# Moving four token normalisations from VectorE to ScalarE in a two-layer transformer kernel

## What is computed

```
def _layernorm(x, axis=-1, eps=1e-05):
    m = jnp.mean(x, axis=axis, keepdims=True)
    v = jnp.var(x, axis=axis, keepdims=True)
    return (x - m) / jnp.sqrt(v + eps)

x = x + _L0_attn_ref(_layernorm(x), ...)   # 16 heads of 8, gated relative position bias
x = x + _L0_ffn_ref(_layernorm(x), ...)    # router, 4 of 16 experts, and a shared expert
x = x + _L1_attn_ref(_layernorm(x), ...)   # 8 heads of rank 64
x = x + _L1_ffn_ref(_layernorm(x), ...)    # feed-forward with FP4-rounded x and weights
```

## Time and profile before

| what | value |
|---|---|
| runs | 2324.96, 2321.24, 2319.95 us |
| median | 2321.24 us |
| profiled execution: its time | 2319.1 us |
| profiled execution: its span | 2317.3 us |
| granted TensorE clock, mean | 0.947 of full speed |
| busy, share of the span | PE 88%, DVE 70%, ACT 56%, POOL 43% |

### The profile page before, as it was taken

The page is one execution under the profiler, slowest core; times in us unless marked ns, Lnnn a source line. Parts: engine busy times, 40 slices in busy tenths (PEclk is TensorE's granted clock), DMA queues, the critical chain, the costliest instruction groups (busy, mean ns, idle before and its releaser), DMA issues. The chain is left out here.

```text
span 2317.3 us, 56731 instructions
## 1 busy us (share of the span) xinstructions
PE 2037.8 (88%) x18115; PEld 1061.5 (46%) x18115; DVE 1625.4 (70%) x3414; ACT 1308.5 (56%) x2072; POOL 1000.9 (43%) x867
## 2 busy tenths in 40 slices
PE   5569999999999999983999759999999999998566
PEld 3434444444444444453555323444444444443345
DVE  4778888888888888866544676666666666664696
ACT  2236666666666666642222346777778787877121
POOL 1133222322322332421000226787878787877454
PEclk9779999999999999976999988999999999999787
DMA  5522212221222221100000271111111111100000
GB/s 134 149 62 56 53 48 53 54 50 50 55 52 48 54 54 49 37 11 1 1 0 0 92 232 36 42 31 38 34 34 37 31 38 31 41 14 1 1 14 23
DMA packets 126924, 106.60 MB, mean 46 GB/s; under 512 B 39636, under 2 KB 102724, under 8 KB 126860
## 3 DMA queue, kind: packets, MB, share of 16 engines
q1 hardware_dynamic: 124640, 103.37, 16.8%
q10 hardware_dynamic: 2220, 2.45, 0.4%
HBM read 75.81 MB, written 29.53 MB: 45 GB/s over the span
## 5 line engine op out<-in xcount | busy, mean ns | idle before, releaser
L1049 DVE TENSOR_REDUCE b_mx<-psum 128x1 f32<-128x512 f32 x1024 | 663.9, 686 | 143.3 <-PE psum L868 81.0
L1033 ACT ACTIVATE b_prob<-psum 128x1024 f32<-128x1024 f32 x512 | 523.9, 1023 | 317.9 <-PE psum L900 317.8
L1736 POOL TENSOR_TENSOR f_plo<-f_prob,f_phi 128x512 f16<-128x512 f32 x512 | 586.5, 1156 | 164.4 <-ACT f_phi L1861 140.1
L1879 DVE TENSOR_REDUCE f_mx<-psum 128x1 f32<-128x512 f32 x512 | 328.7, 683 | 169.1 <-PE psum L1756 168.1
L1860 ACT ACTIVATE f_prob<-psum 128x512 f32<-128x512 f32 x512 | 307.3, 600 | 150.8 <-PE psum L1767 149.7
L948 PE MATMUL psum<-b_prob,b_v 128*32 128x256 f32 x4096 | 327.4, 391 | 1.6 <-ACT b_prob L1033 0.5
L1861 ACT ACTIVATE f_phi<-psum 128x512 f16<-128x512 f32 x512 | 306.0, 598 | 0.0
L804 POOL COPY b_v<-v 128x64 f32 x64 | 15.1, 236 | 596.1 <-PE psum L948 595.7
L900 PE MATMUL psum<-b_diag,b_toep 128*128 128x79 f16 (+1 forms) x4224 | 266.6, 208 | 0.0
L807 POOL TENSOR_TENSOR b_diag<-flip,grev 128x1024 f16<-128x1024 f16 x128 | 239.6, 1892 | 0.0
L900 PEld LDWEIGHTS psum<-b_diag,b_toep 128*128 128x128 f16 x4224 | 235.2, 99 | 9.0 <-issue 2.6
(11 more groups left out here) (301 smaller groups left out, 3432.4 us busy)
## 6 DMA issues: line engine op xcount, KB each, us to landing
d_qk<-e_qk SPq DMA_DIRECT2D x64, 256.0 KB, 2.6
b_toep<-d_line SPq DMA_DIRECT2D x128, 64.0 KB
f_qa<-d_qk SPq DMA_DIRECT2D x64, 128.0 KB, 2.9
f_ka<-d_qk SPq DMA_DIRECT2D x64, 128.0 KB, 2.9
b_q<-d_q SPq DMA_DIRECT2D x128, 54.0 KB
d_k<-a_qk SPq DMA_DIRECT2D x48, 128.0 KB, 2.3
b_toep<-d_line SPq DMA_DIRECT2D x128, 32.0 KB
b_q<-b_m SPq DMA_DIRECT2D x256, 1.0 KB
```

The source lines that it names most:

```text
L1033: nc.scalar.activation(prob[:, t % 4, :].rearrange("p (a n) -> p a n", a=2), ps[:, EXP + 2 * (t % 2):EXP + 2 * (t % 2) + 2, :], ACT.Exp).t ...
L1049: nc.vector.tensor_reduce(mx[:, b, t, half:half + 1], ps[:, bank, :], AX.X, ALU.max).then_inc(s.max_read, 1)
L1736: nc.gpsimd.tensor_tensor(plo[:, t % 4, at], prob[:, t % 4, at], phi[:, t % 4, at], ALU.subtract).then_inc(s.plo_ready, 1)
L1879: nc.vector.tensor_reduce(mx[:, b, t, half:half + 1], ps[:, MAX + half, :], AX.X, ALU.max).then_inc(s.max_read, 1)
```

## The change

The statistics stay on DVE. POOL forms, beside rstd, a shift of -mean * rstd (two more products of 128 x 4). ACT applies the normalisation as one ACTIVATE with the function Identity per tile, with rstd as scale and shift as bias, both per partition: rstd * x + shift. DVE's four TENSOR_SCALARs per chunk go. `norm_stats` gets a wait before it overwrites `mv`, `norm_rstd` one before it overwrites rstd and shift. A third constant row (-1.0) is set once.

```
 def norm_stats(nc, ln, x, n, u, link, dve, rstd_ready, var_ready):
     for k in reversed(range(CT)):
         last = nc.vector.bn_stats(...)
     link(last)
+    dve.wait_ge(rstd_ready, done(n - 2))
     nc.vector.memset(ln.gap[:, :], 0.0)

 def norm_rstd(nc, g, ln, pool, n, u, s):
     pool.wait_ge(s.var_ready, done(n))
+    pool.wait_ge(s.xn_ready, done(n - 2))
     nc.gpsimd.tensor_tensor(ln.rstd[:, u, :], ln.mv[:, u, :, 1], g.lnc[:, 0, :], ALU.add).then_inc(s.eps_added, 1)
+    nc.gpsimd.tensor_tensor(ln.shift[:, u, :], ln.mv[:, u, :, 0], g.lnc[:, 2, :], ALU.mult)
     pool.wait_ge(s.eps_added, done(2 * n))
     nc.gpsimd.tensor_tensor(ln.rstd[:, u, :], ln.rstd[:, u, :], g.lnc[:, 1, :], ALU.pow).then_inc(s.eps_added, 1)
+    pool.wait_ge(s.eps_added, done(2 * n + 1))
+    nc.gpsimd.tensor_tensor(ln.shift[:, u, :], ln.shift[:, u, :], ln.rstd[:, u, :], ALU.mult).then_inc(s.rstd_ready, 1)

-def norm_apply(nc, ln, x, n, u, xn_ready):
+def norm_apply(nc, ln, x, n, u, act, rstd_ready, xn_ready):
+    act.wait_ge(rstd_ready, done(n))
     for k in range(CT):
-        last = nc.vector.tensor_scalar(ln.xn[:, u, k, :], x[...], ln.mv[:, u, k, 0:1], ln.rstd[:, u, k:k + 1], ALU.subtract, ALU.mult)
+        last = nc.scalar.activation(ln.xn[:, u, k, :], x[...], ACT.Identity,
+                                    bias=ln.shift[:, u, k:k + 1], scale=ln.rstd[:, u, k:k + 1])
     last.then_inc(xn_ready, 1)

 # phase_project0, ACT (and apply(n + 1, 1 - u) gone from DVE's step)
+                act.wait_ge(g.x_loaded, 16)
+                apply(0, 0)
                 move_xT(0, 0)
                 def step(n, u, last):
+                    if not last:
+                        apply(n + 1, 1 - u)
                     act.wait_ge(s.gates_psum, done(n))

 # phase_output0
-                pipeline(act, [(4, move_xT), (1, move_aT), (5, score)])
+                pipeline(act, [(4, move_xT), (1, move_aT), (3, normalise), (5, score)])
-                pipeline(dve, [(2, add_stats), (3, normalise)])
+                pipeline(dve, [(2, add_stats)])

 # phase_project1
-                pipeline(act, [(2, lambda n, u: high(n, u, FIRST)), (1, move_xT), (2, lambda n, u: high(n, u, REST))])
+                pipeline(act, [(1, normalise), (2, lambda n, u: high(n, u, FIRST)), (1, move_xT), (2, lambda n, u: high(n, u, REST))])
-                pipeline(dve, [(1, normalise), (2, lambda n, u: low(n, u, FIRST)), (1, low_xT), (0, stats),
+                pipeline(dve, [(2, lambda n, u: low(n, u, FIRST)), (1, low_xT), (0, stats),

 # phase_quant_ffn (and wait for rstd_ready and norm_apply gone from DVE's quant_x)
+                def normalise(n, u):
+                    act.wait_ge(s.xq_begun, done(n - 2))
+                    norm_apply(nc, ln, g.x, n, u, act, s.rstd_ready, s.xn_ready)
-                pipeline(act, [(2, gates), (4, move_hT), (1, move_xT)])
+                pipeline(act, [(1, normalise), (2, gates), (4, move_hT), (1, move_xT)])
```

More of the change, by code:

```diff
@@ L287, in _ @@
                 nc.vector.memset(g.lnc[:, 1, :], -0.5)
+                nc.vector.memset(g.lnc[:, 2, :], -1.0)
                 nc.vector.memset(ones8[:, :], 1.0).then_inc(tab_chain, 1)
@@ L336, in norm_scratch, with norm_stats @@
     ln.gap = sb("gap", [P, 1])
+    ln.shift = sb("shift", [P, 2, CT])
     ln.xn = sb("xn", [P, 2, CT, E])
     return ln
-def norm_stats(nc, ln, x, n, u, link, var_ready):
+def norm_stats(nc, ln, x, n, u, link, dve, rstd_ready, var_ready):
     for k in reversed(range(CT)):
@@ L350, in norm_stats, with norm_rstd @@
     last.then_inc(var_ready, 1)
[L353 to L358, removed]
-def norm_apply(nc, ln, x, n, u, xn_ready):
+def norm_rstd(nc, g, ln, pool, n, u, s):
+    pool.wait_ge(s.var_ready, done(n))
+    pool.wait_ge(s.xn_ready, done(n - 2))
+    nc.gpsimd.tensor_tensor(ln.rstd[:, u, :], ln.mv[:, u, :, 1], g.lnc[:, 0, :], ALU.add).then_inc(s.eps_added, 1)
+    nc.gpsimd.tensor_tensor(ln.shift[:, u, :], ln.mv[:, u, :, 0], g.lnc[:, 2, :], ALU.mult)
+    pool.wait_ge(s.eps_added, done(2 * n))
+    nc.gpsimd.tensor_tensor(ln.rstd[:, u, :], ln.rstd[:, u, :], g.lnc[:, 1, :], ALU.pow).then_inc(s.eps_added, 1)
+    pool.wait_ge(s.eps_added, done(2 * n + 1))
+    nc.gpsimd.tensor_tensor(ln.shift[:, u, :], ln.shift[:, u, :], ln.rstd[:, u, :], ALU.mult).then_inc(s.rstd_ready, 1)
+def norm_apply(nc, ln, x, n, u, act, rstd_ready, xn_ready):
+    act.wait_ge(rstd_ready, done(n))
     for k in range(CT):
-        last = nc.vector.tensor_scalar(ln.xn[:, u, k, :], x[:, bass.ds(n * CT + k, 1), :].rearrange("p a e -> p (a e)"),
-                                       ln.mv[:, u, k, 0:1], ln.rstd[:, u, k:k + 1], ALU.subtract, ALU.mult)
+        last = nc.scalar.activation(ln.xn[:, u, k, :], x[:, bass.ds(n * CT + k, 1), :].rearrange("p a e -> p (a e)"), ACT.Identity,
+                                    bias=ln.shift[:, u, k:k + 1], scale=ln.rstd[:, u, k:k + 1])
     last.then_inc(xn_ready, 1)
@@ L1593, in _ @@
             def _(dve):
-                credit(dve, s.var_ready, s.xn_ready, s.lo_ready, s.xT_low)
+                credit(dve, s.var_ready, s.lo_ready, s.xT_low)
                 def stats(n, u):
[L1597 to L1603, removed]
+                    norm_stats(nc, ln, g.x, n, u, chain(dve, dchain, n), dve, s.rstd_ready, s.var_ready)
                 def low(n, u, products):
```

55 lines of the change are left out of this document (26 added, 29 removed).

## The result

The changed kernel took 2344.29 us in the median of 4 runs (2334.32 to 2351.62), the kernel before 2323.1 (2319.95 to 2326.06). The ratio is 1.0089, with a 95% interval of 1.0047 to 1.013. The change is slower by 0.9%. I had forecast 2315.7 with a range of 2310 to 2321.5. The profiled execution took 2334.32 us. In the padded kernels they differ again.)

A forecast was written before the change was run, and what follows sets the result against it. DVE was taken to bound only phase_quant_ffn, standing behind POOL's large instructions. Terms 1.2 + 0.3 + 2.3 - 9.3 gave -5.5 us, subtracted from the median 2321.24 for 2315.7, range 2310 to 2321.5.

The forecast's parts named there:

- The sum of the four stages: Whole kernel: the changes in the four touched stages, 1.2 + 0.3 + 2.3 - 9.3, add up to -5.5 us.
- ScalarE's price: Four normalised tiles on ScalarE take 1.55 us, 0.44 more than DVE's 1.11; bounds 1.2 and 2.68.
- ScalarE late in the ring: Rival, casts' window in phase_project1: from 1.6 us for four tiles, delays seven later rounds; up to 2325.9 us, chance 0.06.
- a_, +1.2: phase_project0: only the first store's moment counts, and ScalarE's longer path delays it; +1.2 us, range 0.6 to 2.
- that rival: Rival, first chunk of phase_project0: a table switch costs twice its 1.28 us, first store 2.6 later; 2318.3 us, chance 0.03.
- c_, +0.3: phase_output0: ACT's 1.55 us fit its idle 2.02, POOL's 0.45 delays the first tiles; +0.3 us, range -1 to +1.5.
- e_, +2.3: phase_project1: first two chunks are latency chains, second ring round starts 1.9 us later; +2.3 us, range 1 to 5.
- h_, -9.3: phase_quant_ffn: DVE bounds and is relieved of normalising; -9.3 us, range -12 to -5.
- the wait moves whole: Rival, phase_quant_ffn: L609 or L610 inherits the full wait, rounds stay near 18.5 us; 2323.7 us, chance 0.18.
- the middle between two cases: phase_quant_ffn steady rounds: L607 slips between POOL's instructions or waits (gain 1.4 us); middle 1.65 taken, times 4: -6.6.
- The premise of the sum: Whole kernel: stages follow one another, so the change is the sum of what it does to four of them.

The follow-up runs named there:

- apad64: The changed kernel with 64 inert semaphore clears on ScalarE at the head of the routing stage; median 2324.37 us, ratio 0.9984 to the kernel before.
- pad128: The kernel before with 128 inert semaphore clears on ScalarE at the head of the routing stage; median 2325.41 us, ratio 0.9994.
- best: The kernel before with normalisation on ScalarE in phase_quant_ffn alone, plus 112 clears on TensorE in phase_weights; median 2312.49 us, ratio 0.9933.
- bpe112: The kernel before with only the 112 inert clears on TensorE in phase_weights; 2320.82 us, ratio 0.9956.
- mended: The changed kernel with 64 clears on ScalarE, 112 on TensorE, and GpSimd's attention copy ahead of its normalisation work in phase_output0; median 2314.52 us, ratio 0.9951.
- bpe192: The kernel before with 192 inert clears on TensorE at the head of phase_project0; ratio 1.0049, nine of ten runs between 2337.85 and 2345.95 us.
- pad101: The kernel before with 101 inert semaphore clears on ScalarE at the head of the routing stage; median 2349.1 us, ratio 1.009.
- bpe128: The kernel before with 128 inert clears on TensorE at the head of phase_project0; ratio 0.9998, ten runs between 2328.88 and 2335.90 us.

## Why the prediction was wrong

**The sum of the four stages had the right sign and half the size.** It was to be -5.5 us; the first two profiles give 1.5 + 2.3 + 3.0 - 9.3 = -2.5, and apad64 against pad128 gives -3.0. Term by term:

- *ScalarE's price*: 1.65 us for four tiles, 0.48 each, where I had built 1.55 from a copy and a bias. The rival "ScalarE late in the ring" needed more than 1.6 and had a price per microsecond over it; by that price, nine times the excess, 0.05 over is 0.5 us.
- *a_, +1.2*: +1.5. (The listed steps of ScalarE add up to 49.2, not to 49.3; it changes nothing.) The first store came at 51.02, I had said near 51.3. The load of a table began at 42.74, 0.01 after the copy's end at 42.73, and took 1.28. The Trainium skill, "ScalarE: Activation LUTs", section "What ACT_TABLE_LOAD costs", adds some 1.4 us of draining to a switch; the trace does not agree here, and that rival is out.
- *c_, +0.3*: **wrong in size**. It was +2.3 in the first profiles, with a granted clock of 0.61 before and 0.63 after, and 3.4 to 4.5 between later ones and pad128, whose clock there was 0.68. The step that failed is "ACT's 1.55 fit into its idle 2.02; POOL's added 0.45 delays the first tiles". I had followed GpSimd's added work to the next stage of the ring and not to what is queued behind it on GpSimd, the copy for which TensorE waits.
- *e_, +2.3*: +3.0; 1 to 4 between the other pairs of profiles.
- *h_, -9.3*: -9.3. L607 (now L615) slipped in and L609 (now L617) took the wait over. The round was to be 16.8 us and is 16.9. The rival "the wait moves whole" is out; the round did not stay at 18.5. That both numbers meet so exactly is luck. If L607 slipped in, a round was to give 1.9 us; it slipped in and gave 1.57, and the forecast met that only by taking the middle between two cases. And the stage is 10 to 12 us shorter between other pairs (164.54 in best against 174.84 in bpe112, 164.05 in apad64 against 175.98 in pad128).

**The premise of the sum was wrong.** "Stages follow one another, so the change is the sum of what it does to four of them." Five other phases share one instruction stream per engine with these four. The change put 101 instructions into ScalarE's stream ahead of f_'s loop, and at its new place the loop fetches five packets of code in every pass, where it had fetched none. That is 14 us, more than twice the forecast gain, and no rival of mine had it. The step that failed is this premise, by which f_ stood in the sum at nothing without a reason; the runs showed 14.3 us there. This term is enough to turn the sign: with it taken out (apad64) the ratio is 0.9984 (0.9958 to 1.001), no longer slower and not shown to be faster. With c_'s queue and TensorE's loop mended too it is 0.9951, but the clears on TensorE alone give the kernel before 0.9956, on another chip. b_'s 3.2 us, also at nothing in the sum, stay open (below).

The traces I had held the warning. Rows for q8 and q14 of kind "instruction" stood on the page, and in the kernel before q14 moved nothing in six passes of f_: the loop ran without a fetch, and I did not ask on what that hangs. The Trainium skill, "Runtime: NRT & Kernel Launch", section on instruction fetch mechanics, says that an engine's instruction store is a small queue refilled in blocks, and that a taken branch whose target is no longer in it stalls until the block is fetched. The trace agrees: 2.5 us for such a branch on ScalarE and 4.9 on TensorE, against 0.24 and 0.27. The page gives blocks of 16 KB; TensorE's q8 moves 16 KB a packet (0.54 MB in 33), but ScalarE's q14 moves 8 (0.25 MB in 30), and the measurement decides. With the page's 256 instructions in 16 KB, so 128 in 8 KB (an estimate), 288 instructions need three blocks or four, by where they begin. How many blocks the store holds was not measured. The three ScalarE places tried (+0, +101, +128) and the changed kernel's two (+101, +165) agree with a period of 128 instructions, the bad stretch of which holds +101 and not +37. That the fourth block is what makes the loop fetch is the likely reading of this, not a measured one.

**What stays open.** b_ is some 2 us longer on average in the five profiles with the whole change than in the others, once slow passes are taken out: 902.0 to 905.5 us against 899.6 to 902.8 (904.93 in mended, 901.55 in bpe112). The passes of its loop take 54.06 to 54.10 us instead of 53.97 to 54.02, about 1 us in all, and the rest falls at its ends. No fetch shows in them, and no run was made for it. Why a slow branch of TensorE comes back for one to three passes and then stays away, with the same program, was not tried either. The slow passes explain b_ in the profiled runs; for the spread of the others, which have no trace, they are the likely cause, since it shrank to 3 to 8 us wherever the profile had none by padding (leaving out one run far apart in bpe112 and one in bpe192).

## What to carry to other kernels

- An edit that adds instructions to an engine moves every loop behind it on that engine. Before pricing a change, note which loops of the engine run from its store without a fetch (no "instruction" packets in their stretch), how long their bodies are, and count the instructions that the edit puts ahead of them. Clears in an idle stretch can move such a loop to a better place (64 on ScalarE and 112 on TensorE did here; 64 on TensorE made it worse).
- When an untouched stage changes and its busy times do not, read the rows of the instruction queues, and the idle time put down to "issue", before any theory on memory or the clock.
- A wait and two small operations added to a queue are paid by what stands behind them in that queue. Put the copy that another engine waits for ahead.

## What the runs showed of the hardware that was not expected

- ScalarE's loop of 288 instructions runs with no fetch at one place (before, pad128, apad64) and with five packets of 8 KB and 2.3 us more a pass at another, 101 instructions on (after, pad101).
- TensorE's loop in b_ (877 records of weight loads and sequencer, and 748 products, a pass) has three behaviours by place: at +64 every branch back takes 3.3 to 3.9 us and a pass about 8 us more, at +112, +128 and +192 none does, and at +0 the first nought to three do, at 4.6 to 5.1 us each. Moving it by 112 took the runs of the kernel before from 2318 to 2368 (all but one of 27) to 2319 to 2322 (all but one of 10).
- A semaphore clear costs TensorE 0.12 us in a row of them (bpe128), ScalarE 0.07 (pad128).
